# First half-head block of the first attention: stacking part of q and k on TensorE, angles on GpSimd, first loads in another order

## The chip, the cores and the metric

The kernel runs on one core of a Trainium2 chip. The metric is the device time of one execution in microseconds; the median of the runs stands for a kernel. The engines are named as the profile does: PE (TensorE matmuls), PEld (its weight loads), DVE (VectorE), ACT (ScalarE), POOL (GpSimd), SP (SyncE, which here only issues DMAs).

## The reference

Four layers on x of 4 x 512 x 256 (batch s, tokens, features), with 16 heads of 16 features:

```python
# layer 0: causal attention and a GELU network, gated back into x
h = layernorm(x, gamma1, beta1)
Q, K, V = heads(h @ Wq + bq), heads(h @ Wk + bk), heads(h @ Wv + bv)
attn = softmax(where(causal, Q @ K.T / 4, -inf))
x1 = x + (attn @ V) @ Wo + bo
x2 = x1 + gelu(layernorm(x1, gamma2, beta2) @ W1 + b1) @ W2 + b2
x = x + gate * (x2 - x)
# layer 1: low-rank adapter with an expert chosen by a token; layer 2: GELU network of a chosen expert
# layer 3: conditioned attention with a bias and a mask
scale, shift = split(silu(sin_emb(timestep)) @ W_ada + b_ada)     # sin and cos of timestep / 100 * 4000 * freqs
y = ln(x) * (1 + scale) + shift
q, k, v = heads(y @ Wq + bq), heads(y @ Wk + bk), heads(y @ Wv + bv)
x = x + (softmax(mask(q / 4 @ k.T + bias)) @ v) @ Wo + bo
x = x + (h * sigmoid(1.702 h)) @ W2 + b2     # h = (ln(x) * g2 + beta2) @ W1 + b1
```

## The kernel before

There are eight attentions, four of layer 0 and four of layer 3, in the order of `ATTENTIONS`. Each has 64 units: a unit is one head and one block of 128 query rows. Unit numbers `U` run through all attentions; inside one, the half of the heads `c` changes slowest (units 0 to 31 take heads 0 to 7), then the row block `t` (8 units each), then the head. In layer 0 a unit of block `t` needs only the first `(t + 1) * 128` keys. All engines walk one list of ticks; at tick `U` PE issues the scores of unit `U` (`scores`, L1296, and the causal mask, L1299), the transposes of unit `U - 2` (L1314) and the values of four units (L1328), DVE takes the row maximum (`maxima`, L1079), ACT the exponential (`exponentials`, L765), and the copy of the transposed block goes to DVE or ACT by a small planner (`copy_sides`, L1093 and L776). Negative ticks are the work ahead of the first unit.

The dense work lies beside the units at ticks written by hand: `plan_norm` (statistics L936, the reciprocal root L952 to L962, `h` L977), `plan_turn` (`turn_tokens` L1173 and `hT`, half on ACT, L792, half on DVE, L1008), `plan_qkv`, `plan_ffn` and so on; `BESIDE` says at which tick of each attention which block starts. An engine works through its own list in order, so a wait in one step holds up all behind it.

`plan_qkv` makes q and k, two banks of 128 features at a time (`qk`, i = 0 to 3, L1195; i = 0 and 1 are q and k of heads 0 to 7). A product of two float32 numbers is made from bf16 pieces: `hi` (ACT, L801) rounds the result, `rest_of` (DVE, L1014) is what is left, `mid` (ACT, L806) rounds that, `lo` (DVE, L1020) is the third piece. The three pieces are the rows of `parts[i]`, 16 features a head. `parts_to_dram` (SP, L573) writes them to DRAM, five slots for q and three for k, and `stack` (L523, L525) reads them back so that `qs` and `ks` hold eight groups of 16 rows: all pairs of pieces of one head, along the 128 rows that one matmul sums over. `stack` waits until the parts have landed. For the first half of the first attention it is issued by ACT at tick -6, for all others by SP; the scores of units 0 and 32 of each attention wait for `stack_in`.

`v_rows` (PE, L1205) and `values_out` (DVE, L1029) make v in two halves; `V_BANK` puts the second one into dense bank 0.

Setup work: the first loads are 12 DMAs of SP counted in `load_a`, waited for by SP, ACT, DVE and PE as one; GpSimd writes constants (`consts`), issues 31 DMAs counted in `load_b`, then turns a token into a float (L673) and scales wq and bqk of layer 3 (L676, L678). At tick 10 DVE's `setup_angles` (L889 to L906) computes the angles of the timestep embedding in 23 dependent steps of 128 x 4, and ACT's `setup_sin` waits for them and takes sine (L834) and exponent (L836). `setup_silu`, `setup` and `setup_weights` follow at ticks 20 to 22. PSUM has eight banks: two for scores, two for the transposed blocks, one for the context, three for dense work.

## Time and profile before

| | |
|---|---|
| median of three runs | 1181.55 us (1181.41 to 1184.07) |
| the profiled execution | 1181.24 us |
| its span, first to last instruction | 1179.4 us |
| busy over the span | PE 83%, PEld 56%, DVE 62%, ACT 59%, POOL 38% |
| granted TensorE clock, mean | 0.952 |

The span lacks what lies before the first and after the last instruction, 1.84 us. Busy shares are means over stages that differ; which wait ends last in a stage is read from the chain and the timeline. The trace is cut into windows (how busy was each engine in a stretch), the chain (which step was waited for), and the timeline (instructions in order of time; a row stands for `xN` neighbours of one form, its length from the first start to the last end; in brackets the idle time before it and what ended it).

### The profile page before, as it was taken

The numbers are of one execution on the slowest core, as the hardware profiler recorded it, in microseconds if no ns is written. First come the engines' busy times: TensorE is split into PE (matmuls) and PEld (weight loads), VectorE is DVE, ScalarE is ACT, GpSimd is POOL, SyncE is SP. The second block draws the span as 40 slices with busy tenths as digits, with TensorE's granted clock in tenths as the row PEclk, the third lists the DMA queues.
The fourth block names the chain that finished last, engine by engine and source line by source line (L and its number), as shares of the span: only waits on it lengthen the run. The fifth ranks groups of instructions, "written<-read, shape, count | busy, mean of one in ns | idle before, by whom it ended". The sixth has DMA issues, their size and how long they took to land.

```text
span 1179.4 us, 22071 instructions
## 1 busy us (share of the span) xinstructions
PE 984.0 (83%) x7533; PEld 657.6 (56%) x7620; DVE 730.9 (62%) x1964; ACT 692.0 (59%) x1604; POOL 447.9 (38%) x672
## 2 busy tenths in 40 slices
PE   5377889898789898899799898798896899789768
PEld 2144555556456566556556476465574557557545
DVE  4368774563855747865773657746749864764750
ACT  1356667463655774675666656576654675665731
POOL 8000020000170164563044003955747563884920
PEclk9589999999899999989999999999897999989989
DMA  7857612506044263574734129567383377944600
GB/s 214 210 125 180 110 37 74 107 1 144 23 114 104 56 185 125 151 189 157 149 95 103 45 90 193 174 181 196 121 211 123 108 221 225 222 142 135 224 1 18
DMA packets 118114, 155.83 MB, mean 132 GB/s; under 512 B 12717, under 2 KB 80685, under 8 KB 118005
## 3 DMA queue, kind: packets, MB, share of 16 engines
q1 hardware_dynamic: 111748, 146.26, 47.0%
q10 hardware_dynamic: 4256, 4.19, 1.5%
q0 software_dynamic: 2000, 3.97, 1.3%
q8 instruction: 63, 1.03, 0.4%
q14 instruction: 47, 0.38, 0.1%
HBM read 135.51 MB, written 18.88 MB: 131 GB/s over the span
## 4 chain that ended last, share of the span: by engine, by line
PE 45%; DVE 21%; ACT 15%; issue 9%; DMA 5%; POOL 3%; another core or an unknown queue 1%; SPq 1%; ACTq 0%; DVEq 0%; POOLq 0%
PE bank L1240 14%; PE bank L1229 8%; PE bank L1314 6%; PE bank L1195 5%; PE bank L1328 4%; DVE bias L1085 4%; DVE mrow L1079 3%; DMA bias<-in_fside_Bx16xSxS 3%; PE bank L1296 3%; ACT gT L815 3%; POOL bias L739 3%; ACT bias L768 2%; DVE stats L936 2%; ACT L815 2%; ACT prob L765 2%
## 5 line engine op out<-in xcount | busy, mean ns | idle before, releaser
L739 POOL TENSOR_TENSOR bias<-bias,negmask 128x256 f32<-128x256 f32 x512 | 335.4, 686 | 260.2 <-DMA bias<-in_fside_Bx16xSxS 253.9
L768 ACT ACTIVATE bias<-bias,mrow 128x512 f32<-128x512 f32 x256 | 184.1, 719 | 209.6 <-DVE mrow L1085 208.4
L1085 DVE CUSTOM_DVE_ANT_0 bias<-bank,bias 128x512 f32<-128x512 f32 x256 | 175.2, 687 | 185.6 <-PE bank L1296 94.0
L765 ACT ACTIVATE prob<-bank,mrow 128x128 f32<-128x128 f32 (+3 forms) x256 | 134.7, 527 | 192.9 <-DVE mrow L1079 191.3
L1079 DVE TENSOR_REDUCE mrow<-bank 128x1 f32<-128x128 f32 (+3 forms) x256 | 124.3, 486 | 170.4 <-PE bank L1299 169.2
L1314 PE MATMUL bank<-ident,bias 128*128 128x128 f32 x1024 | 163.2, 284 | 66.6 <-ACT pT L776 49.2
L1296 PE MATMUL bank<-ks,qs 128*128 128x512 bf16 (+3 forms) x425 | 145.5, 343 | 65.8 <-ACT prob L765 36.3
L1314 PEld LDWEIGHTS bank<-ident,bias 128*128 128x128 f32 x1024 | 124.5, 145 | 123.5 <-ACT bias L768 70.1
L1229 PE MATMUL bank<-hT,w 128*128 128x512 f32 x384 | 182.8, 607 | 1.9 <-ACT hT L792 1.0
L1240 PE MATMUL bank<-w,gT 128*128 128x256 f32 x768 | 174.3, 381 | 0.0
L1240 PEld LDWEIGHTS bank<-w,gT 128*128 128x128 f32 x768 | 142.5, 190 | 20.2 <-issue 2.7
L776 ACT ACTIVATE pT<-bank 128x512 f32<-128x512 f32 (+3 forms) x276 | 140.1, 508 | 1.1 <-PE bank L1314 1.1
L1093 DVE COPY pT<-bank 128x512 f32<-128x512 f32 (+3 forms) x236 | 136.0, 576 | 5.8 <-PE bank L1314 5.1
L1296 PEld LDWEIGHTS bank<-ks,qs 128*128 128x128 bf16 x512 | 50.5, 99 | 148.1 <-ACT prob L765 67.9
L1314 PE MATMUL bank<-ident,prob 128*128 128x128 f32 x640 | 118.1, 284 | 14.8 <-ACT pT L776 7.9
L1328 PE MATMUL bank<-pT,va 128*32 128x128 f32 x3328 | 124.3, 287 | 4.5 <-DVE ctxn L1112 3.3
L1328 PEld LDWEIGHTS bank<-pT,va 128*32 128x32 f32 x3328 | 88.0, 114 | 28.1 <-issue 25.7
L1229 PEld LDWEIGHTS bank<-hT,w 128*128 128x128 f32 x384 | 68.4, 195 | 61.5 <-issue 59.8
L1314 PEld LDWEIGHTS bank<-ident,prob 128*128 128x128 f32 x640 | 70.7, 144 | 38.4 <-issue 29.1
L698 POOL TENSOR_TENSOR x<-x,xy 128x256 f32<-128x256 f32 x16 | 13.0, 840 | 153.1 <-DVE h L977 153.1
L709 POOL TENSOR_TENSOR xy<-xy,l2row 128x256 f32<-128x256 f32 x16 | 12.1, 784 | 145.0 <-PE bank L1173 145.0
L815 ACT ACTIVATE gT<-bank,b 128x512 f32<-128x512 f32 x96 | 59.9, 685 | 10.4 <-PE bank L1229 10.0
(152 smaller groups left out, 1131.0 us busy)
## 6 DMA issues: line engine op xcount, KB each, us to landing
bias<-in_fside_Bx16xSxS SPq DMA_DIRECT2D x128, 512.0 KB, 4.5
w<-in_L_cond_W SPq DMA_DIRECT2D x16, 1024.0 KB, 5.6
qs<-q_parts SPq DMA_DIRECT2D x30, 384.0 KB, 10.6
ks<-k_parts SPq DMA_DIRECT2D x30, 384.0 KB, 12.0
q_parts<-parts SPq DMA_DIRECT2D x80, 128.0 KB
k_parts<-parts SPq DMA_DIRECT2D x48, 128.0 KB
w<-in_L_cond_Wi SPq DMA_DIRECT2D x4, 1024.0 KB, 4.9
w<-in_L_cond_Wo SPq DMA_DIRECT2D x4, 1024.0 KB, 5.5
```

What stands on the lines that cost most here:

```text
L739: pool.tensor_tensor(b_n, b_n, negmask[:, t, keys], ALU.add).then_inc(masked, 1)
L765: act.activation(prob_of(U), score_bank[U % 2][:, 0:n], ACT.Exp, bias=mrow[:, U % ROW_RING:U % ROW_RING + 1], accum_out=rsum[:, U % ROW_RI ...
L768: act.activation(prob_of(U), prob_of(U), ACT.Exp, scale=-1.0, bias=mrow[:, U % ROW_RING:U % ROW_RING + 1], accum_out=rsum[:, U % ROW_RING: ...
L776: act.activation(pT[:, U % PT_RING, 0:n // P, :], turn_bank[U % 2][:, 0:n].rearrange("p (k q) -> p k q", q=P), ACT.Identity).then_inc(pt_a, 1)
L1079: v.tensor_reduce(m, score_bank[U % 2][:, 0:n], AX_X, ALU.max, negate=True).then_inc(max_done, 1)
L1085: v.tensor_tensor_reduce(out=prob_of(U), in0=score_bank[U % 2][:], in1=prob_of(U), scale=-1.0, scalar=3e38, op0=ALU.add, op1=ALU.min, accu ...
L1093: v.tensor_copy(pT[:, U % PT_RING, 0:n // P, :], turn_bank[U % 2][:, 0:n].rearrange("p (k q) -> p k q", q=P)).then_inc(pt_v, 1)
L1229: mm = pe.matmul(dense_bank[FF_BANK[j]][:], w1[:, c, j * P:(j + 1) * P], hT[:, c, :], start=c == 0, stop=c == ND - 1)
L1240: mm = pe.matmul(dense_bank[FF_OUT_BANK[t // 2]][:, (t % 2) * D:(t % 2 + 1) * D], gT[:, j, t * P:(t + 1) * P], w2[:, j, :], start=j == 0, ...
L1296: mm = pe.matmul(score_bank[U % 2][:, 0:n], qs[:, hd, t * P:(t + 1) * P], ks[:, hd, 0:n], start=True, stop=l == 1)
L1314: mm = pe.transpose(turn_bank[U % 2][:, k * P:(k + 1) * P], prob_of(U)[:, k * P:(k + 1) * P], ident[:])
L1328: mm = pe.matmul(ctx_bank[32 * j:32 * (j + 1), t % 2 * P:(t % 2 + 1) * P], v_h, pT[:, (GH * w + j) % PT_RING, k, :], start=e == 0 and k == ...
```

## The change

Columns 0 to 255 (`EARLY`) of `qs` and `ks` for heads 0 to 7 of the first attention, which are all that its units 0 to 15 read, no longer pass through DRAM. DVE builds selector matrices of zeros and ones in bf16 from the identity (`selectors`). PE multiplies them with `parts` (`restack`): for each side, each of two heads of a 32-row strip, each of three pieces and each of four strips, one matmul of 32 rows by 128 by 256 columns, 48 in all, into all eight banks. ACT copies the four q banks and DVE the four k banks to `qs` and `ks`. Units 0 to 15 wait for these copies. The other columns go the old way; their stack is issued by SP at tick -2 with half of the columns, and unit 16 (`2 * HH`) waits for it. The second half of heads of q and k moves from ticks -5 to -1 to ticks 2 to 6, its stack from 5 to 11, the second half of v from tick -7 to -3 (it uses one of the banks), and the statistics of batch row 1 from tick 0 to -1.

The angles move to GpSimd, in 25 dependent steps (a fused step becomes two, the two quarters are taken together where possible), straight after the memsets of `va`; ACT's sine and exponent move from tick 10 to -12. The three remaining pairs of constants and the 29 late loads follow the angles. x of batch row 0 is loaded in two halves, on SP's and ACT's queues; the token and the frequencies on ACT's. wv and bv get a counter of their own, as do the indices, and SP's steps wait for the indices only. ACT makes a copy of `ident` into `spread` before anything else, so that its first table is loaded there.

```diff
+PAIRS = [((q0 + j) % 3, (k0 + j) % 3) for _, n, q0, k0 in STACK for j in range(n)]
+EARLY = 2 * P
...
-def plan_qkv(t, s, l):
+def plan_qkv(t, s, l, second=6, late=4):
...
-            u = t + 6 * c
+            u = t + second * c
...
-    at(t + 4, "pe", "v", s, l, 1)
-    at(t + 5, "v", "v", s, l, 1)
+    at(t + late, "pe", "v", s, l, 1)
+    at(t + late + 1, "v", "v", s, l, 1)
...
-STACKS_AT = [(-6, 5)] + [(-28, 4)] * 2 + [(-20, 4)] + [(-28, 4)] * 3 + [(-20, 4)]
+STACKS_AT = [(-2, 11)] + [(-28, 4)] * 2 + [(-20, 4)] + [(-28, 4)] * 3 + [(-20, 4)]
 BESIDE = [
-    [(0, norm(0), 1), (6, qkv0, 1), (24, norm(0), 2)],
+    [(-1, norm(0), 1), (6, qkv0, 1), (24, norm(0), 2)],
...
-        at(UNITS * _a + _t, "a" if _a + _c == 0 else "sp", "stack", _s, _l, _c)
+        at(UNITS * _a + _t, "sp", "stack", _s, _l, _c)
 plan_norm(-20, 0, 0)
 at(-14, "v", "setup_scale")
-qkv0(-14, 0)
-at(10, "v", "setup_angles")
-at(10, "a", "setup_sin")
+qkv0(-14, 0, 13, 8)
+at(-12, "v", "selectors")
+at(-12, "a", "setup_sin")
+for _e in ("pe", "v", "a"):
+    at(-6, _e, "restack")
...
-LOADS_A = 12
-LOADS_B = 9 + 2 * 4 + 6 + 3 + 4 + 1
+LOADS_A = 8
+LOADS_V = 2
+LOADS_B = 7 + 2 * 4 + 6 + 3 + 4 + 1
...
+        spare = bias[:, 3, :, :].rearrange("p h k -> p (h k)")
+        select = spare[:, 0:6 * P].bitcast(BF16).rearrange("p (e x m) -> p e x m", e=2, x=6)
+        ident32 = spare[:, 6 * P:6 * P + 32]
...
+        early_q_bank = [score_bank[0], score_bank[1], turn_bank[0], turn_bank[1]]
+        early_k_bank = [ctx_bank, dense_bank[2], dense_bank[0], dense_bank[1]]
...
+            cols = slice(EARLY if a + c == 0 else 0, S)
             for r, k, q0, k0 in STACK:
                 rows = slice(r * DH, (r + k) * DH)
-                eng.dma_start(qs[rows, hs, :],
-                              q_dram[hs, q0:q0 + k].rearrange("h p d t -> (p d) h t")).then_inc(stack_in[c], 16)
-                eng.dma_start(ks[rows, hs, :],
-                              k_dram[hs, k0:k0 + k].rearrange("h p d t -> (p d) h t")).then_inc(stack_in[c], 16)
+                eng.dma_start(qs[rows, hs, cols],
+                              q_dram[hs, q0:q0 + k, :, cols].rearrange("h p d t -> (p d) h t")).then_inc(stack_in[c], 16)
+                eng.dma_start(ks[rows, hs, cols],
+                              k_dram[hs, k0:k0 + k, :, cols].rearrange("h p d t -> (p d) h t")).then_inc(stack_in[c], 16)
...
-            sp.dma_start(xy[0][:], T["x"][0].rearrange("(t p) d -> p t d", p=P)).then_inc(x_in[0], 16)
+            first = T["x"][0].rearrange("(t p) d -> p t d", p=P)
+            sp.dma_start(xy[0][:, 0:2, :], first[:, 0:2, :]).then_inc(x_in[0], 16)
...
-            sp.dma_start(wv[0][:], T["L0_cond_Wv"].rearrange("(c p) n -> p c n", p=P)).then_inc(load_a, 16)
-            sp.dma_start(bv[0][:], T["L0_cond_bv"].partition_broadcast(P)).then_inc(load_a, 16)
-            sp.dma_start(idx[:, 0:B], T["itok_B_0_15"].unsqueeze(0)).then_inc(load_a, 16)
-            sp.dma_start(idx[:, B:2 * B], T["itok_B_0_7"].unsqueeze(0)).then_inc(load_a, 16)
+            sp.dma_start(wv[0][:], T["L0_cond_Wv"].rearrange("(c p) n -> p c n", p=P)).then_inc(load_v, 16)
+            sp.dma_start(bv[0][:], T["L0_cond_bv"].partition_broadcast(P)).then_inc(load_v, 16)
+            sp.dma_start(idx[:, 0:B], T["itok_B_0_15"].unsqueeze(0)).then_inc(idx_in, 16)
+            sp.dma_start(idx[:, B:2 * B], T["itok_B_0_7"].unsqueeze(0)).then_inc(idx_in, 16)
...
                 sp.wait_ge(setup_v, SETUP_V)
+                sp.wait_ge(early_k, 4)
...
-            sp.wait_ge(load_a, 16 * LOADS_A)
+            sp.wait_ge(idx_in, 32)
...
-            late(tok_i, T["itok_B_34_63"].partition_broadcast(P))
-            late(freq, T["freqs"].unsqueeze(1))
+            const(pool.memset(va[0][:], 0.0))
+            const(pool.memset(va[1][:], 0.0))
+
+            n_setup = [0]
+
+            def step(ins):
+
+                n_setup[0] += 1
+                ins.then_inc(setup_p, 1)
+                pool.wait_ge(setup_p, n_setup[0])
+
+            r = lambda i: sin_t[:, i, :]
+
+            def scaled(dst, src, factor, addend):
+                step(pool.tensor_scalar(r(24), src, factor, None, ALU.mult))
+                step(pool.tensor_tensor(dst, r(24), addend, ALU.add))
+
+            pool.wait_ge(angle_in, 32)
+            step(pool.tensor_copy(r(0), tok_i))
+            step(pool.tensor_scalar(r(2), r(0), 0.01, None, ALU.mult))
+            scaled(r(3), r(2), -64.0, r(0))
+            scaled(r(4), r(2), -32.0, r(3))
+            scaled(r(5), r(2), -4.0, r(4))
+            scaled(r(1), r(5), 0.01, r(2))
+            step(pool.tensor_scalar(r(2), r(1), 4000.0, None, ALU.mult))
+            step(pool.tensor_scalar(r(3), r(2), freq, None, ALU.mult))
+            two = lambda i: sin_t[:, i:i + 2, :]
+
+            def less(dst, src, factor, addend):
+                step(pool.tensor_scalar(two(14), src, factor, None, ALU.mult))
+                step(pool.tensor_tensor(dst, two(14), addend, ALU.add))
+
+            for i in range(2):
+                step(pool.tensor_scalar(r(4 + i), r(3), 1.0 / TWO_PI, 0.25 * i, ALU.mult, ALU.add))
+            step(pool.tensor_scalar(two(6), two(4), ROUND, None, ALU.add))
+            step(pool.tensor_scalar(two(8), two(6), ROUND, None, ALU.subtract))
+            less(two(10), two(8), -PI_HI, r(3).unsqueeze(1).broadcast_to([P, 2, B]))
+            less(two(4), two(8), -PI_MID, two(10))
+            less(two(10), two(8), -PI_LO, two(4))
+            for i in range(2):
+                step(pool.tensor_scalar(r(4 + i), r(10 + i), 0.25 * i * TWO_PI, PI_LIMIT, ALU.add, ALU.min))
+            step(pool.tensor_scalar(two(12), two(4), -PI_LIMIT, None, ALU.max))
+            assert n_setup[0] == SETUP_ANGLES
...
-            pool.tensor_copy(sin_t[:, 0, :], tok_i).then_inc(setup_p, 1)
-            pool.wait_ge(setup_p, 1)
-
-            pool.tensor_scalar(wq[1][:], wq[1][:], 0.25, None, ALU.mult).then_inc(setup_p, 1)
-            pool.wait_ge(setup_p, 2)
-            pool.tensor_scalar(bqk[1][:, 0:4:2], bqk[1][:, 0:4:2], 0.25, None, ALU.mult).then_inc(setup_p, 1)
-            pool.wait_ge(setup_p, 3)
+            step(pool.tensor_scalar(wq[1][:], wq[1][:], 0.25, None, ALU.mult))
+            step(pool.tensor_scalar(bqk[1][:, 0:4:2], bqk[1][:, 0:4:2], 0.25, None, ALU.mult))
+            assert n_setup[0] == SETUP_P
...
+            def restack():
+                act.wait_ge(early_q, 4)
+                for g in range(4):
+                    act.activation(qs[:, 2 * g:2 * g + 2, 0:EARLY], early_q_bank[g][:].rearrange("p (h t) -> p h t", h=2),
+                                   ACT.Identity).then_inc(early_q_done, 1)
...
-                act.wait_ge(setup_v, SETUP_ANGLES)
+                act.wait_ge(setup_p, SETUP_ANGLES)
...
+            act.dma_start(xy[0][:, 2:4, :], T["x"][0].rearrange("(t p) d -> p t d", p=P)[:, 2:4, :]).then_inc(x_in[0], 16)
+            act.dma_start(tok_i, T["itok_B_34_63"].partition_broadcast(P)).then_inc(angle_in, 16)
+            act.dma_start(freq, T["freqs"].unsqueeze(1)).then_inc(angle_in, 16)
+            act.wait_ge(consts, CONST_IDENT)
+            act.activation(spread[:, 0:P], ident[:], ACT.Identity)
...
-            def setup_angles():
...
+            def selectors():
+
+                v.wait_ge(consts, CONST_IDENT)
+                link(v.memset(select, 0.0))
+                link(v.tensor_reduce(ident32, ident[:].rearrange("p (g c) -> p c g", c=32), AX_X, ALU.add))
+                for r, parts_of in enumerate(PAIRS):
+                    for side, x in enumerate(parts_of):
+                        v.tensor_copy(select[:, :, 3 * side + x, r * DH:(r + 1) * DH],
+                                      ident32.rearrange("p (e d) -> p e d", e=2)).then_inc(select_done, 1)
+
+            def restack():
+                v.wait_ge(early_k, 4)
+                for g in range(4):
+                    v.tensor_copy(ks[:, 2 * g:2 * g + 2, 0:EARLY],
+                                  early_k_bank[g][:].rearrange("p (h t) -> p h t", h=2)).then_inc(early_k_done, 1)
...
-                    v.wait_ge(x_in[s], 16)
+                    v.wait_ge(x_in[s], 16 if s else 32)
...
                     v.wait_ge(consts, CONSTS)
+                    v.wait_ge(load_v, 16 * LOADS_V)
...
+                if ATT[s, l] == 0:
+                    pe.wait_ge(load_v, 16 * LOADS_V)
+                    if i:
+                        pe.wait_ge(early_k_done, 4)
...
+            def restack():
+                pe.wait_ge(lo_done, 2)
+                pe.wait_ge(v_done, 2)
+                pe.wait_ge(select_done, 2 * len(PAIRS))
+                for side, banks, signal in ((0, early_q_bank, early_q), (1, early_k_bank, early_k)):
+                    for e in range(2):
+                        for x in range(3):
+                            for g in range(4):
+                                rows = slice(32 * g, 32 * (g + 1))
+                                mm = pe.matmul(banks[g][:, e * EARLY:(e + 1) * EARLY], select[rows, e, 3 * side + x, :],
+                                               parts[side][rows, x, 0:EARLY], start=x == 0, stop=x == 2)
+                                if x == 2 and e == 1:
+                                    mm.then_inc(signal, 1)
...
-                if U % (UNITS // 2) == 0:
+                if U == 0:
+                    pe.wait_ge(early_q_done, 4)
+                    pe.wait_ge(early_k_done, 4)
+                if U == 2 * HH or U % (UNITS // 2) == 0 and U:
...
-SETUP_ANGLES = SETUP_SCALE + 5 + 2 + 2 * 8
-SETUP_SILU = SETUP_ANGLES + 3
+SETUP_ANGLES = 2 + 4 * 2 + 2 + 2 + 2 + 3 * 2 + 2 + 1
+SETUP_P = SETUP_ANGLES + 2
+SETUP_SILU = SETUP_SCALE + 3
```

## Rows read from the trace of the kernel before

**Rows 1.** The page: the span, and the chain by engine.

```profile
span 1179.4 us, 22071 instructions
...
PE 45%; DVE 21%; ACT 15%; issue 9%; DMA 5%; POOL 3%; another core or an unknown queue 1%; SPq 1%; ACTq 0%; DVEq 0%; POOLq 0%
```

**Rows 2.** Windows: stretch; PE, PEld, DVE, ACT, POOL busy; granted clock, DMA share.

```profile
28.00:47.00 19.00, 0.00 (x0) 0.00 (x0) 2.76 (x4) 2.53 (x4) 1.91 (x3) 0.55 0.81 170
...
52.00:56.00 4.00, 3.84 (x20) 2.95 (x18) 2.76 (x12) 2.06 (x10) 0.00 (x0) 0.50 1.07 297
```

**Rows 3.** The chain that ended last, to 49 us: start, length in us.

```profile
12.55 1.28 ACT L792
...
20.81 1.74 PE bank L1205 x8
...
36.57 10.71 DMA ks<-k_parts
...
47.82 0.29 DVE mrow L1079
...
48.11 0.66 DVE stats L936 x2
```

**Rows 4.** Timeline to 40 us: start, length, engine, line, tiles, count.

```profile
14.68 3.78 PE L1195 MATMUL bank<-hT,wq 128*128 128x512 f32 x4 [2.23 <-ACT hT L792]
...
18.50 0.69 ACT L801 ACTIVATE parts<-bank,bqk_all 128x512 bf16<-128x512 f32 x1 [3.87 <-PE bank L1195]
...
22.64 0.76 DVE L1029 TENSOR_TENSOR va<-bank,bv 128x256 f32<-128x256 f32 x2 [0.33 <-PE bank L1205]
...
23.32 1.28 DVE L1020 TENSOR_TENSOR parts<-gT,parts 128x512 bf16<-128x512 f32 x2
...
24.20 1.88 PE L1195 MATMUL bank<-hT,wq 128*128 128x512 f32 x4
...
37.12 1.26 ACT L801 ACTIVATE parts<-bank,bqk_all 128x512 bf16<-128x512 f32 x2 [14.13 <-issue]
```

**Rows 5.** Timeline of GpSimd: last of 29 late loads, and small steps.

```profile
26.14 0.54 POOL L632 DMA_DIRECT2D bv<-in_L_cond_bv  x1
...
30.92 0.19 POOL L673 CAST bias<-bias 128x4 f32<-128x4 int32 x1 [4.24 <-DMA bv<-in_L_cond_bv]
...
31.20 1.51 POOL L676 TENSOR_SCALAR wq<-wq 128x512 f32<-128x512 f32 x1
```

**Rows 6.** Timeline of ACT: the exponentials of units 0, 10, 11, 16 and 32.

```profile
48.15 0.37 ACT L765 ACTIVATE prob<-bank,mrow 128x128 f32<-128x128 f32 x1 [8.24 <-DVE mrow L1079]
...
60.10 0.47 ACT L765 ACTIVATE prob<-bank,mrow 128x256 f32<-128x256 f32 x1 [1.82 <-DVE mrow L1079]
...
67.44 0.47 ACT L765 ACTIVATE prob<-bank,mrow 128x256 f32<-128x256 f32 x1
...
75.07 0.58 ACT L765 ACTIVATE prob<-bank,mrow 128x384 f32<-128x384 f32 x1 [1.13 <-DVE mrow L1079]
...
105.10 0.37 ACT L765 ACTIVATE prob<-bank,mrow 128x128 f32<-128x128 f32 x1
```

**Rows 7.** Timeline around the angles, 59 to 67 us.

```profile
59.67 1.88 PE L1195 MATMUL bank<-hT,wk 128*128 128x512 f32 x4
...
59.98 0.16 DVE L891 TENSOR_SCALAR bias<-bias 128x4 f32<-128x4 f32 x1
...
64.66 0.21 ACT L834 ACTIVATE bias<-bias 128x8 f32<-128x8 f32 x1 [2.69 <-DVE bias L906]
...
64.89 1.28 ACT L836 ACT_TABLE_LOAD   x1
...
66.30 1.25 ACT L801 ACTIVATE parts<-bank,bqk_all 128x512 bf16<-128x512 f32 x2
```

**Rows 8.** The chain at 109 us (values), and the timeline at 55 us.

```profile
109.11 1.01 PE bank L1328 x32
...
55.46 0.42 PE L1296 MATMUL bank<-ks,qs 128*128 128x256 bf16 x1
```

47 lines of the change are left out of this document (17 added, 30 removed).

## Prediction

> **What bounds the kernel now.** I read the page first. No engine is full over the span, and the chain that ended last changes hands between PE, DVE and ACT with 9% in which nothing was waited for [rows 1]. So the kernel is a relay of dependent steps, ordered by the tick loop, and an interval taken out of the relay should shorten it one for one, as long as what follows isn't tied to something else. Next the windows of the first 60 us: between 28 and 47 us PE and PEld are at 0.00, ACT and DVE have four instructions each, and the DMA engines are busy (0.81); the granted clock is 0.55 there and 0.50 (the 1.2 GHz level) from 52 to 56 us [rows 2]. The chain names the cause: q and k parts go to DRAM and come back as stacked rows. The last of these transfers takes 10.71 us and lands at 47.28, and only then does the first maximum run, at 47.82 [rows 3]. The change takes the first 16 units off that round trip. After that I looked for what else in the first attention stands in the way: the exponentials of units 10 and 11 start at 60.10 and 67.44, where neighbours are 1 to 2 us apart [rows 6], and the rows between them are two table loads and the angles [rows 7].
>
> **Before the stacking.** Three edits act here. (a) ACT copies `ident` early, so its first table load leaves the path: before, it ran at 12.55 for 1.28 us between the transposes and `hT` [rows 3]. QK can then start about 13.4 instead of 14.68, 1.3 us sooner. But the first four QK matmuls run at half rate (3.78 us, later four take 1.88 [rows 4]), and if the step up comes at the same time as before, some of that is given back: I take 1.1. (b) The load of x is cut over two queues; nothing shows a lone half, so I allow 0.5 us either way, taken as 0. `load_a` no longer waits for wv, bv and idx; DVE's scaling ran straight after `h` anyway, so 0. (c) DVE builds the selectors after `hT`: 18 instructions, by the 0.16 us of a small one [rows 7] 2.9 us, done before the first `hi` could reach DVE (18.50 + 0.69 before, 1.1 less now [rows 4]), so covered; without that cover up to 2 us. The step "lo 1" ended at 24.60 [rows 4]; it now ends at 23.5.
>
> GpSimd's chain lies beside that. 25 dependent small steps replace DVE's 23; the nearest rows are the 0.19 us of a small GpSimd instruction and 0.09 us to the one that waits for it [rows 5], so 25 x 0.28 = 7.0 us. Its start is the landing of two tiny loads behind x on ACT's queue, which I put at 6.5 us. End about 13.5. ACT then has the sine and the exponent, each with a table load, 1.28 + 0.21 + 1.28 + 0.21 = 3.0 us [rows 7] from 13.4, so it is done by 16.5; the first `hi` needs a QK result at 18.50 - 1.1 = 17.4. Covered, with 1 us to spare. Queued behind that wait on ACT are all `hi` and with them everything. Behind the angles on GpSimd stand the last constants (`consts`, wanted by `va` at about 21.5) and the late loads: the last of 29 was issued at 26.14, and GpSimd waited 4.24 us for it [rows 5]. They begin when the constants are done, some 8 us later than before (the chain and the wait for its loads), so the last lands near 39 and the scaling (1.51 us) ends near 41. They are wanted at tick 16, by my sum about 55 us. Costs nothing.
>
> On the table loads the rows show 0.02 us between the end of the sine (64.87) and the load (64.89), and its end (66.17) is followed by the exponent and, at 66.30, by `hi` [rows 7]. The Trainium skill, "ScalarE: Activation LUTs", section "What ACT_TABLE_LOAD costs", adds a drain of about 1.38 us to every switch of sets. By that rule the two switches would end about 2.8 us later, an estimate; the trace disagrees, and the mechanism is a rival below.
>
> **The stacking itself.** PE: 2 sides x 2 x 3 x 4 = 48 matmuls on 32 rows, 256 columns of bf16, each with a weight load of 128 columns. No row has this form. From below: four tiles of the array in use at once, as in the values, where 32 matmuls take 1.01 us [rows 8], gives 48 x 0.032 = 1.5 us. From above at full clock: one after the other, each at half of the 0.42 us that a matmul of this width took at the lower clock, 48 x 0.21 = 10 us [rows 8]. The values' row is nearest, since here too four consecutive matmuls go to four separate strips and four banks; their weight loads are four times as wide, so 2.5 us. The Trainium skill, "TensorE: Matmul & The Clock Gate", section "Part 3: Packing small matmuls — row/col tiling", gives 3.07x for four row tiles; by it the 48 would take 48 x 0.107 / 3.07 = 1.7 us, an estimate, 0.8 less than my term.
>
> Then DVE copies the k banks, by ACT's copies of the same size (0.63, two in 1.26 [rows 4]) and DVE's 0.64 (two in 1.28, [rows 4]) 4 x 0.6 = 2.4 us; ACT's q copies (2.5) start when half of the matmuls are done and end before. Next is the late half of `v`, held back for the bank: 8 matmuls, 1.74 us [rows 3], on PE ahead of the first scores, and 0.76 us of `va` on DVE [rows 4], and then the first two statistics of the next batch row, 0.66 us, which stood behind the first maximum [rows 3]. Sum: 23.5 + 2.5 + 2.4 + 1.9 + 0.8 + 0.7 = 31.8 for the first maximum, against 47.82: **-16.0**. The statistics moved ahead are saved behind it: **-0.7**.
>
> **The first 16 units.** The restarted PE finds a gap of some 2.5 us instead of 19, so I expect 2.4 GHz instead of 1.2. From 52 to 56 us PE was busy for 3.84 of 4.00 us at the lower level [rows 2]; at the higher one that work takes half, 1.9 us less where PE is what the relay waits for and nothing where it isn't: **-1.0** (0 if the gap is enough for the clock to fall, then +1.7 for the `v` matmuls too). The angles: ACT's next useful work after unit 10, `hi`, began at 66.30; its input, the QK matmuls, was there at 61.55, so the stall is worth 4.75, and DVE's 23 steps (from 59.98) lie inside it [rows 7]: **-4.7** (-3 to -5.6). Against this stands the second half of q and k, which ran inside the idle time (from 24.20, and again from 37.12 [rows 4]) and now runs at ticks 2 to 6: PE 2 x 1.88 = 3.8, ACT two `hi` in 1.26 and as much for `mid`, DVE two `lo` in 1.28 and as much for `rest` [rows 4]. If the engines take turns it costs 8.9, if only PE counts 3.8; the relay hides part, as PE's own next units do: **+5.0**.
>
> At unit 16 the rest of the columns must be there. Parts are issued from 23 us; with 8 issues and a transfer they land near 33 (1.1 us before the 34 of before), their stack is issued by SP at once and took 10.71 us from last issue to landing with twice the bytes [rows 3]: at most 47, against unit 16 near 56 (75.07 before [rows 6]). The SP queue is blocked till 33, then free for w1, w2 and the expert, earlier than before. The second half's parts leave at about 43 to 48, land by 54, SP stands in the stack's wait till then, and even at 10 to 15 us more this is 70 against unit 32 at 88. `early_k` ahead of the first bias loads is long met. Sum: -16.0 - 0.7 - 1.0 - 4.7 + 5.0 = **-17.4**.
>
> Nothing later depends on a fixed time, so this carries to the end: span 1179.4 - 17.4 = 1162.0. The profiled run was 1181.24, 1.84 above its span, and the median 0.31 above that: 1164.2, said as **1164**.
>
> **Rivals.** (1) GpSimd's chain is late: if a dependent step costs 0.55 rather than 0.28 us, it ends at 20.3, sine and exponent by 22, `hi` waits near 5 us: 1169. For: one pair of rows is thin ground for 25 steps [rows 5]. (2) ACT stands still behind each switch of tables, say once more as long as the load itself: 13.4 + 3.0 + 2 x 1.28 = 19.0 against 17.4, `hi` 1.6 us late, 1166. Against: the 0.02 us of [rows 7]. This is what the drain of the Trainium skill's page named above would do. (3) The stacking runs one by one (+7.5), 1171; or the stack for unit 16 lands late, since the late loads and 2 MB of w1 and w2 now run beside it: 5 to 10 us of stall, 1169 to 1174. Against: 9 us of slack. (4) Slower than before: the strips do not overlap and PE is at 1.2 GHz, where a matmul of this width takes 0.42 us [rows 8], and with a weight load of a third of that in front, since nothing overlaps, 0.56. 48 x 0.56 = 27 us instead of 2.5, +24.5: 1188. From 0.42 us a matmul (20 us in all) the gain is gone, from 0.49 it is slower by 0.3%. Against: PE has just worked for 10 us and its QK matmuls were at the higher rate by 24.20 [rows 4]. (5) The freed time comes back: a later wait sits where the ticks 2 to 16 were, and no more than 3 us is left: 1179. Nothing in the rows holds such a wait.
>
> **How the numbers follow.** Forecast 1164 with 0.63; (1) 0.11; (2) 0.05; (3) 0.13; (4) 0.04; (5) 0.04. The forecast's own bounds: 1.5 us of stacking and 3.8 for the added half give 1162, an x that lands earlier and more clock 1159; 4 us more for the second half and a fallen clock give 1171. Range 1158 to 1174, which leaves (4), (5) and the worst of (3) outside. About 0.3%, 3.5 us, is what a measurement can tell: faster 0.92 (forecast and rivals 1 to 3), same 0.04 (5), slower 0.04 (4).
>
> **What would show it.** The first maximum near 32 us; 48 matmuls in 1.5 to 10 us between 23 and 34; no wait of ACT's first `hi` on anything but PE; no idle time on the stack's DMA at units 16 and 32; units 10 to 11 within 2 us; unit 16's exponential near 57 to 58, unit 32's near 88, and that distance held to the end. The forecast is wrong if the strips do not overlap, if GpSimd's steps are slow, or if the half of q and k inside ticks 2 to 6 costs near 8.9.

## The result, and the profile after

| | before | after |
|---|---|---|
| median | 1181.7 us (1181.41 to 1184.07) | 1165.32 us (1163.56 to 1168.42) |
| the profiled execution | 1181.24 us | 1163.56 us |
| its span | 1179.4 us | 1161.5 us |
| first maximum | 47.82 us | 30.82 us (timeline) |
| exponentials of units 0 / 16 / 32 | 48.15 / 75.07 / 105.10 | 31.13 / 57.97 / 87.26 |

The time is 0.9847 of before (95% interval 0.9824 to 0.9870), 16.4 us less; 1164 was forecast. Line numbers below are those of each kernel's own file: L1258 is QK (L1195 before), L1272 the v matmuls, L1367 the stacking, L1142 the maxima, L824 the exponentials. First the page, against [rows 1]:

```profile
span 1161.5 us, 22288 instructions
...
PE 51%; DVE 18%; ACT 15%; issue 9%; DMA 4%; POOL 4%; DVEq 0%; ACTq 0%; POOLq 0%
```

PE's share of the chain rose from 45 to 51% and DMA's fell from 5 to 4%. The chain itself, 17 to 35 us (start, length, what), in place of [rows 3]:

```profile
17.35 1.74 PE bank L1272 x8
...
21.23 2.02 PE bank L1367 x48
...
25.95 3.42 PE bank L1272 x8
...
30.24 0.66 DVE stats L998 x2
...
30.90 0.20 DVE mrow L1142
...
32.04 3.06 PE bank L1258 x4
```

There is no DMA between 17.35 and the first maximum any more: v, the stacking, a stretch in which DVE copies k (23.3 to 25.9), v's second half, and the work at tick 2. The timeline of the same time with what lies beside it (start, length, engine, line, tiles, count, idle time before), in place of [rows 4, 5]:

```profile
6.27 0.17 DVE L1014 TENSOR_SCALAR norm_rows_t<-mv 128x4 f32<-128x4 f32 x1
...
6.41 0.19 POOL L675 CAST bias<-bias 128x4 f32<-128x4 int32 x1 [2.06 <-DMA bias<-in_freqs]
...
9.94 0.43 DVE L951 TENSOR_SCALAR wq<-wq 128x512 f32<-128x512 f32 x1
...
12.18 3.46 PE L1258 MATMUL bank<-hT,wq 128*128 128x512 f32 x4 [1.03 <-ACT hT L851]
...
14.34 0.27 POOL L698 TENSOR_SCALAR bias<-bias 128x8 f32<-128x8 f32 x1
...
14.63 0.21 ACT L899 ACTIVATE bias<-bias 128x8 f32<-128x8 f32 x1 [1.28 <-POOL bias L698]
...
16.27 0.67 ACT L860 ACTIVATE parts<-bank,bqk_all 128x512 bf16<-128x512 f32 x1
...
19.89 1.28 DVE L1082 TENSOR_TENSOR parts<-gT,parts 128x512 bf16<-128x512 f32 x2
...
21.23 2.02 PE L1367 MATMUL bank<-parts,bias 32*128 32x256 bf16 x48 [2.15 <-DVE parts L1082]
...
22.19 2.06 ACT L893 ACTIVATE qs<-bank 128x512 bf16<-128x512 f32 x4 [2.67 <-PE bank L1367]
...
23.36 2.48 DVE L968 CAST ks<-bank 128x512 bf16<-128x512 f32 x4 [2.19 <-PE bank L1367]
...
25.95 3.40 PE L1272 MATMUL bank<-wv,hT 128*128 128x256 f32 x8 [2.71 <-issue]
```

Read it in three places. DVE's first small step of the reciprocal root (6.27) is 0.17 us. GpSimd's chain runs from 6.41 to 14.61, and ACT's sine follows at 14.63. DVE's last copy of k ends at 25.84, and only 0.1 us later v's second half starts. The windows (stretch, busy us of PE, PEld, DVE, ACT, POOL, granted clock, DMA share), against [rows 2]:

```profile
21.00:22.00 1.00, 0.77 (x28) 0.74 (x32) 0.17 (x1) 0.00 (x0) 1.00 (x2) 1.00 0.22 55
22.00:23.00 1.00, 1.00 (x28) 0.60 (x16) 0.00 (x0) 0.81 (x2) 1.00 (x3) 0.52 0.55 109
...
24.00:28.00 4.00, 2.05 (x5) 1.72 (x6) 1.85 (x4) 0.25 (x1) 4.00 (x7) 0.50 0.73 183
...
52.00:56.00 4.00, 4.00 (x30) 3.02 (x31) 3.74 (x10) 3.38 (x11) 0.00 (x0) 1.00 0.36 125
```

PE is busy where it stood still for 19 us, and from 52 to 56 us it is granted 1.00 where it was 0.50 before. But the clock falls to the lower level, 1.2 GHz, at about 22.0 us, in the midst of the stacking: PE had stood still for 2.15 us (19.08 to 21.23, until `lo` was there) and had then worked for 0.8 us at 1.00. The second time that it stands still, 2.71 us from 23.25, comes after the fall, and the clock is still low for v's second half. ACT's exponentials of units 0, 8, 10, 11, 16 and 32, against [rows 6]:

```profile
31.13 0.37 ACT L824 ACTIVATE prob<-bank,mrow 128x128 f32<-128x128 f32 x1 [6.87 <-DVE mrow L1142]
...
44.38 0.48 ACT L824 ACTIVATE prob<-bank,mrow 128x256 f32<-128x256 f32 x1
...
48.02 0.47 ACT L824 ACTIVATE prob<-bank,mrow 128x256 f32<-128x256 f32 x1 [2.49 <-DVE mrow L1142]
...
50.13 0.47 ACT L824 ACTIVATE prob<-bank,mrow 128x256 f32<-128x256 f32 x1
...
57.97 0.58 ACT L824 ACTIVATE prob<-bank,mrow 128x384 f32<-128x384 f32 x1 [1.19 <-DVE mrow L1142]
...
87.26 0.37 ACT L824 ACTIVATE prob<-bank,mrow 128x128 f32<-128x128 f32 x1
```

From unit 10 to unit 11 it is 2.11 us, where it was 7.34. Unit 0 comes 17.0 us earlier, unit 16 17.1, unit 32 17.8, and the span is 17.9 shorter.

### The profile page after: what moved, and what is told of

It reads as the page before. It is cut to its first block, busy times and chain, and to the rows that moved or that the text cites. A ratio compares the mean times of both kernels' runs of the same rounds, so it can differ in the third digit from the quotient of the medians.

```text
span 1161.5 us, 22288 instructions
## 1 busy us (share of the span) xinstructions
PE 997.7 (86%) x7668; PEld 658.7 (57%) x7668; DVE 730.8 (63%) x1964; ACT 694.2 (60%) x1608; POOL 454.1 (39%) x694
## 4 chain that ended last, share of the span: by engine, by line
PE 51%; DVE 18%; ACT 15%; issue 9%; DMA 4%; POOL 4%; DVEq 0%; ACTq 0%; POOLq 0%
PE bank L1307 14%; PE bank L1296 9%; PE bank L1399 7%; PE bank L1258 5%; PE bank L1413 5%; PE bank L1381 4%; POOL bias L798 4%; DMA bias<-in_fside_Bx16xSxS 3%; DVE mrow L1142 3%; ACT gT L874 3%; DVE bias L1148 3%; ACT bias L827 2%; ACT prob L824 2%; ACT L874 2%; ACT L827 2%
## 5 line engine op out<-in xcount | busy, mean ns | idle before, releaser
L824 ACT ACTIVATE prob<-bank,mrow 128x128 f32<-128x128 f32 (+3 forms) x256 | 134.7, 527 | 193.1 <-DVE mrow L1142 191.6
L1142 DVE TENSOR_REDUCE mrow<-bank 128x1 f32<-128x128 f32 (+3 forms) x256 | 124.5, 488 | 164.5 <-PE bank L1384 163.1
L1381 PE MATMUL bank<-ks,qs 128*128 128x512 bf16 (+3 forms) x512 | 180.3, 352 | 49.2 <-ACT prob L824 34.5
```

The lines of the kernel that those rows point to most:

```text
L824: act.activation(prob_of(U), score_bank[U % 2][:, 0:n], ACT.Exp, bias=mrow[:, U % ROW_RING:U % ROW_RING + 1], accum_out=rsum[:, U % ROW_RI ...
L1142: v.tensor_reduce(m, score_bank[U % 2][:, 0:n], AX_X, ALU.max, negate=True).then_inc(max_done, 1)
L1381: mm = pe.matmul(score_bank[U % 2][:, 0:n], qs[:, hd, t * P:(t + 1) * P], ks[:, hd, 0:n], start=True, stop=l == 1)
```

## The experiments

All kernels compute the whole reference. Times are medians, and differences are taken between kernels that were measured side by side where they can be, since the median of before itself moved from 1181.7 to 1184.0. The two numbers behind a ratio are its 95% interval. The theory is the recorded sum: an interval taken out of the relay ahead of unit 0 or between units comes off the end one for one. Its rival is that only one of the parts counts.

**1. The memsets alone.** What I had not expected in the trace was that `h` started at 8.65 instead of 9.89. In before, GpSimd filled `va` from 4.46 to 7.28, beside DVE's root, and then one row of `eT`; the timeline of before there:

```profile
5.90 1.38 POOL L643 MEMSET va<- 128x1536 f32 x1
...
6.05 1.25 DVE L952 TENSOR_SCALAR norm_rows_t<-mv 128x4 f32<-128x4 f32 x1
...
7.33 0.52 POOL L644 MEMSET eT<- 1x512 f32 x1
...
7.33 0.55 DVE L954 TENSOR_SCALAR norm_rows_t<-norm_rows_t 128x4 int32<-128x4 int32 x1
```

```diff
+            const(pool.memset(va[0][:], 0.0))
+            const(pool.memset(va[1][:], 0.0))
             late(tok_i, T["itok_B_34_63"].partition_broadcast(P))
...
-            const(pool.memset(va[0][:], 0.0))
-            const(pool.memset(va[1][:], 0.0))
```

> The kernel before with one edit: GpSimd fills va (two memsets of 1.38 us) ahead of everything but ident, where it did so between 4.46 and 7.28 us, beside DVE's statistics and reciprocal root. Theory A (DVE's small steps were held up by GpSimd's memsets beside them, not by their own work): the first step of the root falls from 1.25 to about 0.2 us and the second from 0.55 to 0.2, h starts 1.2 to 1.5 us earlier (8.4 to 8.7 instead of 9.89), and the first maximum comes 1.2 to 3 us before 47.82; time 1178.5 to 1180.5. Rival B (the step was slow by itself, as the first of its kind): root unchanged, h at 9.9, time within 1 us of before.

Measured 1183.73 beside 1182.89 for before (ratio 1.0003, 0.9988 to 1.0018): no gain. Timeline of DVE, and the QK matmuls from the chain:

```profile
6.13 0.17 DVE L952 TENSOR_SCALAR norm_rows_t<-mv 128x4 f32<-128x4 f32 x1
...
8.70 1.38 DVE L977 TENSOR_SCALAR h<-xy,mv,norm_rows_t 128x256 f32<-128x256 f32 x4
...
11.32 0.43 DVE L883 TENSOR_SCALAR wq<-wq 128x512 f32<-128x512 f32 x1 [1.25 <-DMA idx<-in_itok_B]
...
14.16 6.62 PE bank L1195 x8
```

The mechanism of A is there: the first step of the root takes 0.17 instead of 1.25 us and `h` starts at 8.70. In before the two slow steps ended with the memsets beside them (7.30 and 7.28, 7.88 and 7.85). But the scaling of wq, which before followed `h` at once, now waits for the last of the 12 first loads until 11.32. QK still starts 0.5 us earlier (14.16 against 14.68), but takes 6.62 instead of 6.13 us and ends at 20.78 against 20.81. From there on nothing is gained, and the trip through DRAM, 0.9 us longer in this profile, puts the first exponential at 48.99. So the 1.2 us were lost in two places, and only the first of them is met by the shorter `load_a`. The time that A gave was wrong.

**2. Everything but the stacking.**

```diff
-STACKS_AT = [(-2, 11)] + [(-28, 4)] * 2 + [(-20, 4)] + [(-28, 4)] * 3 + [(-20, 4)]
+STACKS_AT = [(-6, 5)] + [(-28, 4)] * 2 + [(-20, 4)] + [(-28, 4)] * 3 + [(-20, 4)]
...
-qkv0(-14, 0, 13, 8)
-at(-12, "v", "selectors")
+qkv0(-14, 0)
...
-for _e in ("pe", "v", "a"):
-    at(-6, _e, "restack")
```

(and all columns in the first stack, on ACT's queue, with the waits that go with it)

> The changed kernel without its stacking on PE: all columns go through DRAM, issued as before, second half of q and k, v and statistics at their old ticks, no selectors. Angles on GpSimd, split loads and early table load stay. Theory A (the recorded sum, corrected by the trace: start 3.4 us earlier, 5.2 us at unit 11): first maximum at 44 to 45 us, unit 16's exponential at 66 to 67, time about 1173. Theory by the sum as recorded (1.1 at the start, 4.7 at the angles): 1175.9. Rival B (the angles cost nothing in the units' relay, all gain is the stacking): 1178 to 1181.

Measured 1180.87 (ratio 0.9991, 0.9975 to 1.0007), against 1182.89. So without the stacking some 2 of the 16.4 us are left. Neither sum holds. The time lies where rival B put it, but not for B's reason, for the angles do give their 5.2 us. The chain and a window of 28 to 47 us say why:

```profile
25.82 8.93 DMA k_parts<-parts
...
37.88 12.38 DMA ks<-k_parts
...
28.00:47.00 19.00, 0.00 (x0) 0.00 (x0) 2.76 (x4) 2.53 (x4) 9.66 (x15) 0.53 0.98 213
```

The parts left 3.4 us earlier than before (the first was issued at 20.72 instead of 24.08), but took 8.93 us from the last issue to landing, where it was 5.11, and the stack 12.38 where it was 10.71 [rows 3]. It landed at 50.26, 3.0 us later than before, with the DMA engines at 0.98 where they were at 0.81 [rows 2]. The exponential of unit 0 was at 51.13 and units 10 to 11 took 2.11 us: +3.0 and -5.2 make -2.2. By the medians the kernel is 2.0 us faster than before, which is not clear of noise.

**3. The late loads ahead of the angles again**, otherwise as 2. All 25 steps of the angles move behind the last issue.

```diff
-            pool.wait_ge(angle_in, 32)
-            step(pool.tensor_copy(r(0), tok_i))
...
             late(bv[1][:], T["L3_cond_bv"].partition_broadcast(P))
+            pool.wait_ge(angle_in, 32)
+            step(pool.tensor_copy(r(0), tok_i))
...
-at(-12, "a", "setup_sin")
+at(10, "a", "setup_sin")
```

> The kernel without early stacking (no_early_stack) with GpSimd's 29 late loads issued ahead of the angles instead of behind them, and sine and exponent at tick 10 again. In no_early_stack the parts left 3.4 us earlier than before, yet the stack landed 3 us later. Theory A (the late loads, pushed 8 us back by the angles, ran beside the parts' trip through DRAM and slowed it): now the parts land in about 5 us instead of 8.9, the first maximum is near 44.5 instead of 50.8, and with the angles still off DVE the time is 4 to 7 us below no_early_stack's 1180.9, 1174 to 1177. Rival B (a trip through DRAM that starts earlier meets the loads of x and w instead): the first maximum stays at 48 to 51, time 1179 to 1182.

Measured 1178.12 (ratio 0.9961, 0.9940 to 0.9982), where experiment 2 had 0.9991: by the ratios 3.5 us less, between the two forecasts and with intervals that still overlap. Chain and window:

```profile
27.12 6.22 DMA k_parts<-parts
...
35.83 10.76 DMA ks<-k_parts
...
28.00:47.00 19.00, 0.27 (x3) 0.30 (x4) 2.76 (x4) 2.52 (x4) 5.53 (x19) 0.52 0.79 167
```

The parts take 6.22 us, the stack 10.76, the DMA share is 0.79, and the exponential of unit 0 is at 47.47, 3.7 us ahead of experiment 2. From the first issue of parts to the landed stack it is 24.3 us, where experiment 2 had 29.5 and before 23.2. So the late loads beside the trip through DRAM made it slower, as A has it. The first maximum (47.14) came later than the 44.5 expected, because the parts took 6.2 us and not 5, and because the QK matmuls of this execution took 6.74 us instead of 5.23, so that the first parts left only at 22.28. And part of the stall is back:

```profile
60.02 1.28 ACT L895 ACT_TABLE_LOAD   x1
...
61.54 1.28 ACT L897 ACT_TABLE_LOAD   x1
...
62.95 1.25 ACT L856 ACTIVATE parts<-bank,bqk_all 128x512 bf16<-128x512 f32 x2
```

ACT's two table loads and two functions hold it from 60.02 to 62.95 though the angles were done. Units 10 to 11 take 4.65 us. So of the 5.2 us of the stall about half was the wait for DVE's chain and half the tables.

**4. The angles back on DVE at tick 10**, all else as changed.

```diff
+at(10, "v", "setup_angles")
+at(10, "a", "setup_sin")
-at(-12, "a", "setup_sin")
-            step(pool.tensor_scalar(r(2), r(0), 0.01, None, ALU.mult))
...
+            def setup_angles():
...
```

> The changed kernel with the angles again on DVE at tick 10 and sine and exponent on ACT there. Theory A (the stall of ACT behind the angles is worth 4.7 to 5.2 us, whatever precedes it): first maximum within 0.5 us of 30.8, the gap from unit 10 to unit 11 is again 7 us instead of 2, and the time is 4.5 to 5.5 us above the changed kernel. Rival B (with the second half of q and k now just ahead, the stall hides part): 1 to 3 us above. Rival C (GpSimd's early chain cost something at the start too): less than 4 because the first maximum comes earlier.

1173.44, 8.1 us above the first measurement of the changed kernel; too much for A, but the two were not measured side by side. So once more, beside it:

> The kernel angles_back once more, now beside the changed kernel. In its first profile it was 5.2 us late at unit 32 against changed_again, yet its median lay 8 us higher, in another call. Theory A (5 us is the price of the stall, the rest was spread between calls and the clock's phase): 4 to 6.5 us above the changed kernel. Rival B (the angles on DVE cost something more later on): 7 us or more above.

1173.59 (ratio 0.9931, 0.9905 to 0.9957) against 1168.58 for the changed kernel beside it (0.9884, 0.9856 to 0.9912): 5.0 us, theory A. The intervals just touch, but the trace shows the 5 us where they should be, 7.32 us from unit 10 to 11 instead of 2.12:

```profile
48.26 0.47 ACT L795 ACTIVATE prob<-bank,mrow 128x256 f32<-128x256 f32 x1 [2.48 <-DVE mrow L1137]
...
55.58 0.47 ACT L795 ACTIVATE prob<-bank,mrow 128x256 f32<-128x256 f32 x1
```

**5. The changed kernel twice more, beside the others.**

> The changed kernel once more, beside the others of this call. By the spread so far (1163.56 to 1168.42) its median is 1163 to 1167. Theory A (the step of PE's clock during the first QK matmuls falls at another time in each execution): the eight QK matmuls, 5.18 us in the first profile, take between 5.2 and 6.7, and the first maximum moves with them, up to 1.5 us. Rival B (the spread comes from later stages): the first maximum is within 0.3 us of 30.8.

1165.77 (1164.28 to 1169.29), ratio 0.9848.

> The changed kernel, as the base for the two others of this call: 1163 to 1168. In the trace unit 32's exponential is between 87 and 91 us, as in its first two profiles (87.26 and 90.43), and the distance to before at the last unit is 15 to 18 us.

1168.58 (1165.25 to 1172.08), ratio 0.9884. The first maximum was at 30.82, 30.94 and 31.09 us in the three profiles of this kernel, so the start is steady in them, as B has it; other kernels whose code is the same up to there took up to 6.70 us for the QK matmuls (v_before_stack), so A's range occurs too. What moves in the three is the stretch from unit 0 to 16: 26.8, 28.8 and 27.1 us, with units 8 to 10 at 3.6, 5.1 and 3.6. PE runs four QK matmuls in this stretch; in the first profile and in changed_again:

```profile
44.88 2.47 PE L1258 MATMUL bank<-hT,wq 128*128 128x512 f32 x4
...
45.29 3.75 PE L1258 MATMUL bank<-hT,wq 128*128 128x512 f32 x4
```

From 44 to 48 us the mean granted clock is 0.76 in the first and 0.50 in the second. In every profile of this document these four matmuls and units 8 to 10 go together: 1.95 us with 3.1, 2.47 with 3.6, 3.75 with 5.1. So the clock decides this stretch. It does not explain the spread of the times: changed_again, 3.2 us behind the first profile at unit 32, has a span 2.7 us longer, and changed_third, 0.6 us behind at unit 32, one 7.2 us longer.

**6. The order of the stacking.**

```diff
-                    for e in range(2):
-                        for x in range(3):
-                            for g in range(4):
+                    for g in range(4):
+                        for e in range(2):
+                            for x in range(3):
```

> The changed kernel with the 48 matmuls of the stacking in another order: all six of one strip behind one another, where four strips took turns. Theory A (42 ns a matmul because four strips run at once; in one strip each waits for the one before): 48 x 0.107 = 5.1 us or more instead of 2.0, the first maximum 3 us later, time 3 us above the changed kernel. Rival B (the rate is set by something else, such as issue or the weight loads): 2 to 2.5 us, time unchanged.

```profile
21.17 3.72 PE L1367 MATMUL bank<-parts,bias 32*128 32x256 bf16 x48 [2.15 <-DVE parts L1082]
```

3.72 us instead of 1.80 in the changed kernel beside it: 78 against 38 ns a matmul. A part of this is the clock, whose mean over these matmuls was 0.61 against 0.79. If their time goes with the clock, 47 against 30 ns would be left at 1.00, an estimate. So strips that take turns are quicker by their order alone, which is what the lower bound of the prediction rested on, but a strip alone is quicker than the 0.107 us that A took. The first exponential was 1.8 us later (33.03 against 31.24), the time 1169.11 against 1165.77. Yet by unit 8 the two profiles were level (44.61 and 44.79): here the clock had risen again by the QK matmuls at tick 2, which took 1.88 us instead of 3.00. The two spans are level too (1164.1 and 1164.2), and the intervals of the ratios overlap (0.9855 to 0.9918, 0.9822 to 0.9875): the 1.8 us at the start are shown, their way to the end is not.

**7. The stacking made twice.**

```diff
-                for side, banks, signal in ((0, early_q_bank, early_q), (1, early_k_bank, early_k)):
+                for rep, side, banks, signal in [(rep, *z) for z in ((0, early_q_bank, early_q), (1, early_k_bank, early_k)) for rep in range(2)]:
-                                if x == 2 and e == 1:
+                                if x == 2 and e == 1 and rep:
```

> The changed kernel with each side's 24 matmuls of the stacking made twice, 96 in all, the signals on the second pass. Theory A (the stacking lies on the path one for one): first maximum 2.0 us later (32.8), time 2 us above the changed kernel. Rival B (a busier PE keeps the clock up, so that v and the first units are faster): first maximum later by less than 2 us, since v's 8 matmuls take 1.8 instead of 3.4, and the time unchanged or up to 1.5 us lower.

```profile
21.96 2.80 PE L1367 MATMUL bank<-parts,bias 32*128 32x256 bf16 x96 [2.15 <-DVE parts L1082]
```

96 take 2.80 us, 29 ns each, at a granted clock of 1.00 (windows of 20 to 24 us; in changed_again 0.80), so the second pass costs 1.0 us and not 2.0. Unit 0's exponential is at 33.00, 1.8 us later than 31.24: 1.0 from here, and 0.6 because `lo` ended that much later. The time is 3.1 us above, 1168.91, with overlapping intervals. B is wrong: v's second half took 3.75 us. The clock stayed at 1.00 through the longer stacking, but fell at about 26.8 us, in the time in which PE stood still behind it (24.76 to 27.47). So both of these gaps matter, the one ahead of the stacking and the one behind it.

**8. v ahead of the stacking.** The longest step on the path that the prediction had at the wrong size was v's second half: 3.4 us.

```diff
-qkv0(-14, 0, 13, 8)
+qkv0(-14, 0, 13)
-                    if i:
-                        pe.wait_ge(early_k_done, 4)
-                pe.wait_ge(v_done, 2)
...
+                    if side:
+                        pe.wait_ge(v_done, 4)
```

> The changed kernel with the second half of v made right behind the first one, ahead of the stacking; only the k side of the stacking waits for its bank to be read. In the changed kernel v's 8 matmuls stand between DVE's last copy and the first scores and take 3.4 us at the lower clock, plus 0.76 us on DVE. Theory A (these 4 us are on the path): first maximum near 27, 3.5 to 4.2 us before 30.8, time 3 to 4.5 us below the changed kernel, some 1160 to 1162. Rival B (the gap left on PE is then longer, the clock stays at the lower level for longer, and half is given back): 1 to 2.5 us below.

1164.78 (ratio to before 0.9841, 0.9820 to 0.9863). The changed kernel was not measured beside it and had 0.9847, 0.9848 and 0.9884, so the two can't be told apart by the time.

```profile
22.58 1.53 PE L1366 MATMUL bank<-parts,bias 32*128 32x256 bf16 x48 [0.25 <-DVE parts L1082]
...
27.30 0.27 DVE L1142 TENSOR_REDUCE mrow<-bank 128x1 f32<-128x128 f32 x1
...
28.37 3.57 PE L1258 MATMUL bank<-hT,wq 128*128 128x512 f32 x4
```

The first maximum is 3.5 us earlier, at 27.30, as A says. v's second half now fills the gap ahead of the stacking, and the clock was at 1.00 through it. But PE stood still for 2.8 us while DVE copied k, the clock fell at about 28.3, and the four QK matmuls at tick 2 took 3.57 us. At unit 32 (86.26) the kernel is 1.0 us ahead of the first profile of the changed kernel, 1.6 ahead of the third and 4.2 ahead of changed_again. The last is the one whose units 8 to 10 took as long (5.1 us). So how much is given back depends on which execution it is held against, and B is not shown.

**9. The same with PE kept at work.**

```diff
+                pe.wait_ge(early_q_done, 1)
+                for _ in range(18):
+                    pe.transpose(score_bank[0][:, 0:P], ident[:], ident[:])
```

> The second half of v ahead of the stacking, and 18 transposes of ident on PE, whose result nobody reads, into a bank that ACT has emptied, while DVE copies k. Theory A (v ahead of the stacking lost 2.5 of its 3.5 us because PE stood still for 2.6 us and ran the first units' work at 1.2 GHz): the four QK matmuls at tick 2 take 1.9 instead of 3.6 us, unit 16 comes 25 to 26.5 us after unit 0 instead of 28.3, and the time is 1.5 to 3 us below that of v_before_stack, 1161 to 1163. Rival B (the loss lies in the units' own waits or the loads beside them): unit 0 to unit 16 stays at 28, time 1164 to 1166.

1160.78 (all runs 1158.14 to 1163.90), beside 1165.77 for the changed kernel (1164.28 to 1169.29) and 1183.96 for before: ratio to before 0.9804 (0.9778 to 0.9830).

```profile
24.00 2.19 PE L1372 MATMUL bank<-ident 128*128 128x128 f32 x18
...
27.10 0.28 DVE L1142 TENSOR_REDUCE mrow<-bank 128x1 f32<-128x128 f32 x1
...
28.16 1.88 PE L1258 MATMUL bank<-hT,wq 128*128 128x512 f32 x4
```

18 transposes of which nothing is read, in a stretch in which PE had no work, and the four matmuls take 1.88 instead of 3.57 us; the windows show a granted clock of 1.00 from 20 to 36 us (0.73 from 36 to 40, 0.50 from 40 to 44). A's time holds; of its other figures, unit 16 comes 27.2 us after unit 0 instead of 28.3, not 25 to 26.5, since the next QK matmuls ran at the lower level again (3.75 us). The two edits of 8 and 9 together beat the changed kernel by 5.0 us. What the transposes alone give is less clear. Against v_before_stack the traces show 1.3 us at unit 16 and 0.8 at unit 32 (85.42 and 86.26), and 1.2 at the 191st exponential of layer 0, near 380 us. The rest of the 4.4 us between the two spans comes after that, in stretches that this edit does not touch. The two were not measured side by side, and the intervals of their ratios overlap.

**10. The statistics at tick 0 again**, on top of 9 (one number in `BESIDE`, -1 to 0).

> v_before_warm_pe with the statistics of batch row 1 at tick 0 again instead of -1. Theory A (they only change places with the first maximum): first maximum 0.66 us earlier, near 26.4, unit 2 and all later ones within 0.5 us, time within 1 us of v_before_warm_pe's 1160.8. Rival B (ahead of the first maximum they were on the path and behind it they are hidden): unit 2 and the time 0.7 us earlier or more, which the time alone can't tell.

1161.48, beside 1168.58 for the changed kernel (ratio to before 0.9823, 0.9799 to 0.9847): no difference that these runs can tell from 9. Unit 0 came 0.2 us earlier and not 0.66, unit 2 0.4 earlier. In this profile the granted clock is at 1.00 from 27 to 51 us, units 8 to 10 take 3.1 us, and unit 16 comes 3.4 us ahead of experiment 9 (51.24 against 54.62), unit 32 2.9 us. Yet both spans are 1160.0. One new wait shows on the way:

```profile
54.33 0.69 ACT L860 ACTIVATE parts<-bank,bqk_all 128x512 bf16<-128x512 f32 x1 [2.41 <-DMA q_parts<-parts]
```

ACT's `hi` of the next batch row may overwrite `parts` only when the parts of the second half of heads have landed in DRAM. Here it waits 2.41 us for those of q and then 1.33 for those of k, and PE stands still for 3.33 us, until 57.64. From unit 16 to 32 it takes 31.3 us, where the three profiles of the changed kernel have 29.3 to 30.4. In experiment 9 the same waits are 0.93 and 1.33 us, in the changed kernel there are none. So a start that is earlier still meets the trip through DRAM again. The 2.9 us that are left at unit 32 are lost later on, and these runs don't show to what.

## Why the prediction was right, step by step

It was right in its size (1164 against 1165.3) and in both large mechanisms, the trip through DRAM and the angles. In part it was luck: errors of the sum cancelled, and one of them differs from execution to execution.

- **Ahead of the stacking: 1.1 us forecast, 3.4 measured.** `lo` ended at 21.17, not 23.5. The early table load gave its 1.3 us. Two things were left out. GpSimd's memsets had slowed DVE's small steps, and moving them gave 1.2 us (experiment 1 shows the mechanism). And the QK matmuls took 5.18 us instead of 6.13, where I had expected that an earlier start would give some of it back. These 0.95 us are in part luck: the eleven later profiles of kernels with the same start have 5.2 to 6.7 us, five of them under 5.5, and the 6.13 of before lies in that range. "DVE's scaling ran straight after `h` anyway, so 0" also failed: once `h` is earlier the 12 first loads bind, as experiment 1 shows, so the shorter `load_a` was needed.
- **GpSimd's chain:** 8.2 us instead of 7.0 (0.33 a step), done at 14.61 instead of 13.5. With QK 1.2 us earlier than forecast the cover was just gone: the first `hi` started at 16.27, right behind the exponent, where its QK result was there at 15.6. The chain that ended last doesn't run through it, so no cost is seen. Rival 1 wanted 0.55 a step. Rival 2 did not occur either: the sine ends at 14.84, the table load starts at 14.86 and the exponent at 16.16, so the switch took the 1.28 us of the load. The Trainium skill ("ScalarE: Activation LUTs", "What ACT_TABLE_LOAD costs") adds a drain of about 1.38 us to every switch; this trace disagrees, as in before.
- **The stacking:** 2.02 us against 2.5, copies 2.48 against 2.4. The choice of the values' row was right, and experiments 6 and 7 give 78 ns a matmul for strips one by one and 29 at the full clock.
- **v's second half: 1.74 us forecast, 3.42 measured.** The prediction had the fallen clock as its bound (+1.7) and took the other end. It looked at the gap behind the stacking only, and in the changed kernel the clock had fallen before that gap, 0.8 us after the end of the 2.15 us in which PE waited for `lo`.
- **First maximum:** 31.8 forecast, 30.82 measured; -2.3 ahead of the stacking, -0.5 for it, +0.1 for the copies, +1.7 for the clock.
- **Units 0 to 16:** the sum had -1.0 (clock), -4.7 (angles), +5.0 (second half) and -0.7 (statistics), -1.4 in all; measured -0.1 in the first profile and +1.9 and +0.2 in the others. The angles gave 5.2 in the trace and 5.0 in experiment 4 (the 4.7 was counted from k's QK result at 61.55, but `hi` could have started with q's, there at 59.4). For the second half and the clock together the sum had +4.0. Where the clock was at 1.00 all the way (experiment 10, whose statistics are at the tick of before), units 0 to 8 took 11.0 us, 2.1 more than the 8.8 of before, and units 8 to 10 the same as before. So the second half was sized too high. In the changed kernel the clock was higher on the mean than in before (0.87 against 0.77 over these units), but low where the added QK matmuls ran: those at tick 2 took 2.9 to 3.2 us instead of 1.9, units 0 to 8 took 13.3 to 13.6 and units 8 to 10 another 0.5 to 2.0 us more than in before. The term that failed is the clock.
- **Units 16 and 32** met no DMA wait, so slack was there as forecast, though the parts landed 2.6 us later than I said (the stack was issued from 35.63), 8.6 us behind their last issue where it was 5.1.
- **"This carries to the end"** held in the first profile: -17.0 at unit 0, -17.8 at unit 32, -17.9 for the span. In the two others it was -14.7 and -17.2 at unit 32, and -15.2 and -10.7 for the span: a single pair of profiles can't carry such a statement to better than some 5 us. Rivals 3 to 5 did not occur; strips made to run one by one cost 1.8 us at the start (experiment 6), not 7.5.

What is left open: where the 5 us of spread after unit 32 come from, and why the QK matmuls ahead of unit 0 take anything from 5.2 to 6.7 us. The windows show a granted clock of 1.00 there in all profiles. That a slower DRAM trip follows from the late loads is shown for the kernel without stacking only; in the changed kernel nothing waits for it.

## What to carry to other kernels

Before an edit is costed at nothing because another wait ended last anyway, ask which of two waits will bind once the first is gone: three small edits at the start were worth 2.5 us together, and the one that was tried alone gained nothing at the end. A step that is moved off the path moves the DMA issues queued behind it too, and those can meet a transfer that is still on the path. Where PE stands still for two or three microseconds ahead of dense work, look at the granted clock in fine windows, also behind the gap: here the fall came 0.8 us after PE was at work again, and the gaps ahead of and behind the stacking both counted. Matmuls whose result nobody reads kept it up here and were ahead by about 1 us at unit 32. And compare two profiles unit by unit before a difference of their times is put down to an edit: two executions of the same kernel that were 0.6 us apart at unit 32 ended 7.2 us apart.

## What the runs showed of the hardware that I had not expected

- A small DVE step beside a memset on GpSimd can last until the memset is done: 1.25 us beside one of 128 x 1536 and 0.55 beside one of 1 x 512, against 0.17 and 0.27 us in memsets_first and 0.17 in the changed kernel.
- PE stood still for 2.15 us, worked at a granted clock of 1.00 for 0.8 us and was then granted 0.50 (changed kernel, from about 22.0 us). v's eight matmuls behind it took 3.42 us in place of 1.74, and 3.4 to 3.8 in six profiles (2.89 in a seventh, where the clock fell only in their midst).
- Matmuls on 32 rows with 256 columns: 78 ns each in one strip at a mean granted clock of 0.61; with four strips in turn 42 ns at 0.70, 38 at 0.79, and 29 to 32 at 1.00. Scaled by the clock that is 47 against 30 ns, a factor of about 1.6, an estimate. The Trainium skill, "TensorE: Matmul & The Clock Gate", section "Part 3: Packing small matmuls — row/col tiling", has 3.07x for 512 columns; no run here had 512.
